# Scan over sequence states: a part of the inflow products on GpSimd, and their decays in PSUM

## The chip, the cores and the metric

The program runs on one core of one Trainium2 chip. The metric is the device time of one execution in microseconds. A core has five engines that run their own instruction streams and wait for one another by semaphores: TensorE (PE, with its weight loads as PEld), VectorE (DVE), ScalarE (ACT), GpSimd (POOL) and SyncE (SP), which issues most transfers. All data are fp32. SBUF holds 128 partitions; PSUM has eight banks of 128x512 fp32, which the kernel calls `dense[:, bank, :]`.

## What is computed

The input is x (4 batches, 1024 positions, 1024 channels) and a context (4, 1024, 512). The output is

```
x = x + ssm(ctx, z = layernorm(x))        # state space block
x = x + ffn(layernorm(x))                 # routed experts (top 2 of 8 per batch), then w3
```

The part that matters here is the recurrence of the first block. For each channel e and each of 16 states n, along the 1024 positions t:

```
dA_t    = exp(delta_t * A[e, n])
h_t     = h_(t-1) * dA_t + (delta_t * u_t) * B_t[n]
y_t     = sum over n of h_t * C_t[n]
```

u is a causal convolution of four taps over an input projection, followed by silu. delta is the softplus of a projection of u; B and C are projections of u as well, one row of 1024 positions per state. Then y + D*u is multiplied by silu(z).

## The kernel before, in words

A batch is cut in 16 steps: two halves in time (`th`, 512 positions each) by eight blocks of 128 channels (`j`). A step `g` handles one tile of 128 channels x 512 positions for all 16 states, in eight slots `q` of one pair of states each (2q and 2q+1). The four batches make 64 steps (`g` from 0 to 63) and a tail. The feed-forward work of batch b-1 and the layer norm of the next batch are put into the slots of batch b by a table written out by hand (`Schedule`, lines 61 to 247): each engine's program walks through all slots in order, so the order of the work on an engine is fixed. The diff leaves the table alone.

For each state n of a step the engines do this:

- ScalarE writes `dA = exp(delta*A)` (line 1189) into one of `RA` = 4 buffers in SBUF. It waits until the scan of four states earlier has read that buffer.
- VectorE multiplies `du = delta*u` (a PSUM bank, DU) by the broadcast row of B (`Bb`) into one of two PSUM banks, M0 for even and M1 for odd states (`times_b`, line 1426). In batch 0, ten of the sixteen products are made by TensorE instead; batches 1 to 3 make all sixteen on VectorE.
- VectorE runs the scan over 512 positions (line 1450), from `dA` and the bank, into `h`. In the second half in time it starts from `state`.
- GpSimd multiplies a pair's `h` by `Cb` in place (line 812, once per slot). In the first half it first copies the last column to `state` (line 806).
- TensorE adds the pair into the accumulator bank YT by transposing matmuls (line 905). `h` has three pairs of buffers (`RH`), so the scan of pair q waits until pair q-3 has been summed.

VectorE makes the products of a pair right after the scans of the pair before it. Around that, a step has further work that couples the engines:

- **Convolution.** In slot 1 (slot 2 in the last channel block) ScalarE makes the first tap of the tile ten steps ahead, after the two `dA` of that slot (`tap_one`, lines 1105 to 1115). In the same slot VectorE makes the three other taps (line 1288), the first of them ahead of the slot's scans; it waits for `first_tap`.
- **Delta of the next step.** TensorE makes `v` (line 864) once the last tap has freed bank S. ScalarE runs Abs, Exp and Ln in slot 4 (lines 1133 to 1139); VectorE ends the softplus after the scans of slot 3 (line 1318). GpSimd makes `du_s` = delta*u in slot 4 (line 785), ScalarE copies it to bank DU in slot 7 (line 1145).
- **Gate.** ScalarE normalizes the z tile in slot 3 (line 1204), and in slot 6 loads another activation table, makes silu of u and of z (lines 1121 and 1221) and loads the first table again (line 1156).
- **Experts.** In batches 1 to 3, sixteen slots a batch hold a Gelu of two tiles with a table load ahead and behind (line 1262): slots 0, 2, 4, 6 of steps 5, 6 and 11, slots 4 and 6 of step 10, slots 0 and 2 of step 12. The expert's output is added by VectorE (line 1404) one slot later. Steps are counted within a batch, from 0.
- **w3 and logits.** TensorE's matmuls of lines 1078 and 1055 lie between its other work, most of them in steps 7 to 9 and 12 to 15.

Of the kernel before, what the change touches and what calls it, by code (L numbers as in the profile page):

```python
# [17 lines left out]
N = 16  # L18
# [19 lines left out]
PE_PAIRS = (1, 2, 4, 5, 6)  # L38
TAIL = 240
# [213 lines left out]
def build(nc, x, ctxT, w_inT, conv_w, conv_b, x_projT, dt_projT, dt_b, A_log, D, sw, sw_b,  # L253
# [4 lines left out]
    with ExitStack() as ctx:  # L258
# [43 lines left out]
        duT = sb("duT", [P, 2, TB, P])  # L302
        h = sb("h", [P, 2 * RH, T])
# [104 lines left out]
        duB_pe_done = sem("duB_pe_done")  # L408
        dA_done = sem("dA_done")
# [65 lines left out]
        def vec_index(g, n):  # L475

            return N * g + n - pe_index(g, n)
# [64 lines left out]
        def _(sync):  # L542
# [77 lines left out]
            def reload_bc(g, c, q):  # L620

                if q == 0:
                    e.wait_ge(bc_stored, 1 + 16 * (c + 1))
                e.wait_ge(duB_done, 1 + vec_index(g, 2 * q + 2))
                e.wait_ge(duB_pe_done, 1 + pe_index(g, 2 * q + 2))
                e.wait_ge(prod_done, 1 + 1 + PAIRS * g + q + 1)
                load_bc(c, q)

            def slot(b, t):
# [31 lines left out]
                for what, *a in PLAN.slots[b][t]:  # L661
# [9 lines left out]
                    elif what == "tail_row":  # L671
                        k = a[0]
                        if k >= 2:
                            e.wait_ge(duB_done, 1 + vec_index(ALL - 1, 2 * (k - 1)))
                        load_x1(tail_rows[k], tail_row_loaded[k], NB - 1, TB + 2 + k if k < 2 else k - 2)
# [6 lines left out]
                    elif what == "sw_load":  # L682
# [60 lines left out]
        def _(pool):  # L743
# [36 lines left out]
            def du_of(g, delta_ready):  # L780
# [11 lines left out]
            def slot(b, t):  # L792
# [7 lines left out]
                if b < NB:  # L800
# [13 lines left out]
                    if q == 4 and g + 1 < ALL:  # L814
                        du_of(g + 1, 1 + count(b, "v", st) + 1)
                    if st == STEPS - 2 and q == 4 and b + 1 < NB:
                        edges(b + 1)
# [266 lines left out]
        def _(act):  # L1084
# [89 lines left out]
            def slot(b, t):  # L1174
# [5 lines left out]
                if b < NB:  # L1180
# [18 lines left out]
                    if q == 3:  # L1199
# [8 lines left out]
                    if q == 4 and g + 1 < ALL:  # L1208
# [60 lines left out]
        def _(dve):  # L1269
# [90 lines left out]
            def slot(b, t):  # L1360
# [77 lines left out]
                for n in (2 * q, 2 * q + 1):  # L1438
                    if on_pe(g, n):
                        e.wait_ge(duB_pe_done, 1 + pe_index(g, n) + 1)  # L1440
                    else:
# [8 lines left out]
                    e.tensor_tensor_scan(h[:, 2 * ((PAIRS * g + q) % RH) + n % 2, :], dA[:, (N * g + n) % RA, :], dense[:, product_bank(g, n), :],  # L1450
# [120 lines left out]
```

## Time and profile before

| | us |
|---|---|
| median of 3 runs | 2517.73 (2517.63 to 2517.95) |
| the profiled execution, its own time | 2518.56 |
| its span in the trace | 2516.8 |
| VectorE busy | 2157.6 (86%) |
| TensorE busy | 2025.6 (80%) |
| ScalarE busy | 1545.5 (61%) |
| GpSimd busy | 1444.6 (57%) |

Batch 1 begins at 562.5 us of the span (first scan of step 16), batch 2 at 1157.5, batch 3 at 1746.5; the last step ends near 2290.3, and the tail takes the rest. Busy times are of instructions from start to end; consecutive instructions of VectorE and ScalarE overlap by about a tenth of a microsecond, so the distance between two starts (the pitch) is what one costs in a full queue.

### The profile page before, as it was taken

The numbers are of one execution on the slowest core, as the hardware profiler recorded it, in microseconds if no ns is written. First come the engines' busy times: TensorE is split into PE (matmuls) and PEld (weight loads), VectorE is DVE, ScalarE is ACT, GpSimd is POOL, SyncE is SP. The second block draws the span as 40 slices with busy tenths as digits, with TensorE's granted clock in tenths as the row PEclk, the third lists the DMA queues.
The fourth block names the chain that finished last, engine by engine and source line by source line (L and its number), as shares of the span: only waits on it lengthen the run. The fifth ranks groups of instructions, "written<-read, shape, count | busy, mean of one in ns | idle before, by whom it ended". The sixth has DMA issues, their size and how long they took to land.

```text
span 2516.8 us, 32784 instructions
## 1 busy us (share of the span) xinstructions
PE 2025.6 (80%) x10840; PEld 1205.0 (48%) x10840; DVE 2157.6 (86%) x2788; ACT 1545.5 (61%) x2237; POOL 1444.6 (57%) x990
## 2 busy tenths in 40 slices
PE   6797889976757897996757897897676897895899
PEld 2676676654433553544433454454443454453244
DVE  5899899979998899989999999998999899994210
ACT  2676566656658569645658658855677768852500
POOL 0687677767755556656756655664675566663000
PEclk9899999997878999997878998998787998997799
DMA  5312425564613744566632554565541264566411
GB/s 172 126 43 84 131 72 167 168 193 158 235 35 109 232 155 144 162 210 205 224 111 84 180 173 134 175 206 181 209 168 63 75 214 152 180 218 242 168 59 67
DMA packets 200186, 382.76 MB, mean 152 GB/s; under 512 B 31537, under 2 KB 97073, under 8 KB 200018
## 3 DMA queue, kind: packets, MB, share of 16 engines
q1 hardware_dynamic: 196848, 380.21, 46.0%
q8 instruction: 87, 1.43, 0.2%
q10 hardware_dynamic: 3170, 0.47, 0.1%
q14 instruction: 81, 0.66, 0.1%
HBM read 346.53 MB, written 34.08 MB: 151 GB/s over the span
## 4 chain that ended last, share of the span: by engine, by line
PE 41%; DVE 21%; issue 18%; ACT 13%; POOL 3%; DMA 2%; DVEq 0%; SPq 0%; ACTq 0%; POOLq 0%
PE dense L1078 13%; DVE h L1450 9%; PE dense L905 8%; PE dense L843 5%; ACT dA L1189 4%; DVE dense L1426 4%; PE dense L891 3%; POOL h L812 3%; DVE u L1288 2%; PE dense L855 2%; ACT L1156 2%; PE dense L1008 2%; PE dense L912 2%; ACT L1262 2%; PE dense L864 2%
## 5 line engine op out<-in xcount | busy, mean ns | idle before, releaser
L812 POOL TENSOR_TENSOR h<-h,Cb 128x1024 f32<-128x1024 f32 x512 | 1208.5, 2361 | 429.8 <-DVE h L1450 405.7
L1189 ACT ACTIVATE dA<-delta,Av 128x512 f32<-128x512 f32 x1024 | 705.4, 717 | 449.3 <-DVE h L1450 446.4
L905 PE MATMUL dense<-ident,h 128*128 128x128 f32 x4096 | 602.8, 298 | 179.0 <-POOL h L812 177.6
L905 PEld LDWEIGHTS dense<-ident,h 128*128 128x128 f32 x4096 | 518.4, 154 | 330.5 <-POOL h L812 240.0
L1450 DVE TENSOR_TENSOR_SCAN h<-dA,state,dense 128x512 f32<-128x512 f32 x512 | 628.4, 1267 | 30.5 <-issue 13.4
L1450 DVE TENSOR_TENSOR_SCAN h<-dA,dense 128x512 f32<-128x512 f32 x512 | 597.3, 1205 | 16.5 <-PE dense L905 8.0
L1426 DVE TENSOR_TENSOR dense<-dense,Bb 128x512 f32<-128x512 f32 x864 | 551.9, 685 | 1.6
L1078 PE MATMUL dense<-w3h,xT 128*128 128x512 f32 x832 | 388.9, 601 | 0.0
L806 POOL COPY state<-h 128x2 f32<-128x2 f32 x256 | 47.6, 186 | 356.1 <-DVE h L1450 354.6
L891 PE MATMUL dense<-Bb,duT 128*128 128x128 f32 x1280 | 181.0, 289 | 48.6 <-DVE h L1450 40.6
L1078 PEld LDWEIGHTS dense<-w3h,xT 128*128 128x128 f32 x832 | 148.6, 194 | 129.0 <-issue 129.0
L843 PE MATMUL dense<-ctxs,win 128*128 128x512 f32 x432 | 209.1, 629 | 1.2 <-ACT dtw L1128 0.7
L891 PEld LDWEIGHTS dense<-Bb,duT 128*128 128x128 f32 x1280 | 160.6, 198 | 80.3 <-issue 74.3
L864 PE MATMUL dense<-dtaug,dtw 33*128 33x512 f32 x128 | 91.3, 800 | 112.3 <-DVE u L1288 110.6
L1288 DVE SCALAR_TENSOR_TENSOR u<-dense,cw,u 128x511 f32<-128x511 f32 (+2 forms) x192 | 140.9, 734 | 41.9 <-ACT u L1106 22.7
L1156 ACT ACT_TABLE_LOAD x113 | 145.0, 1283 | 2.0
L1412 DVE TENSOR_TENSOR res<-dense,res 128x512 f32<-128x512 f32 x64 | 44.0, 687 | 118.1 <-PE dense L1078 117.9
L843 PEld LDWEIGHTS dense<-ctxs,win 128*128 128x128 f32 x432 | 84.2, 204 | 100.8 <-issue 100.8
L1008 PE MATMUL dense<-hs,w2s 128*64 128x512 f32 x224 | 74.7, 740 | 45.0 <-ACT hs L1262 44.2
L1055 PE MATMUL dense<-sww,row 128*32 128x256 f32 x1336 | 109.9, 413 | 1.2 <-ACT row L1230 1.0
L1145 ACT COPY dense<-du_s 128x512 f32<-128x512 f32 x64 | 37.6, 587 | 107.3 <-DVE dense L1426 107.3
L864 PEld LDWEIGHTS dense<-dtaug,dtw 33*128 33x128 f32 x128 | 23.1, 225 | 141.1 <-issue 140.9
(151 smaller groups left out, 2035.6 us busy)
## 6 DMA issues: line engine op xcount, KB each, us to landing
sww<-in_sw SPq DMA_DIRECT2D x170, 512.0 KB, 4.3
Cb<-bc_scratch SPq DMA_DIRECT2D x64, 512.0 KB, 5.7
Bb<-bc_scratch SPq DMA_DIRECT2D x54, 512.0 KB, 4.4
w3h<-in_sw SPq DMA_DIRECT2D x54, 512.0 KB, 8.5
w3h<-in_w3T SPq DMA_DIRECT2D x52, 512.0 KB, 5.1
row<-x_scratch SPq DMA_DIRECT2D x42, 512.0 KB, 4.9
xz<-in_x SPq DMA_DIRECT2D x64, 256.0 KB, 5.0
xt<-in_x SPq DMA_DIRECT2D x64, 256.0 KB, 4.1
```

Source lines behind the costliest of these rows:

```text
L812: e.tensor_tensor(h[:, s:s + 2, :], h[:, s:s + 2, :], Cb[:, 2 * q:2 * q + 2, :], ALU.mult).then_inc(prod_done, 1)
L843: mm = e.matmul(dense[:, bank, :], win[:, par, k, :], ctxs[:, k, :], start=(k == 0), stop=(k == DK - 1))
L864: e.matmul(dense[:, S, :], dtw[0:DR + 1, j * P:(j + 1) * P], dtaug[:], start=True, stop=True) \
L891: mm = e.matmul(dense[:, product_bank(g, n), k * P:(k + 1) * P], duT[:, g % 2, k, :], Bb[:, n, k * P:(k + 1) * P], start=True, stop=True)
L905: mm = e.matmul(yT[:, k, :], h[:, 2 * ((PAIRS * g + q) % RH) + i, k * P:(k + 1) * P], ident[:], is_transpose=True, start=False, stop=(q == ...
L1008: mm = e.matmul(dense[HD * i:HD * i + HD, bank, :], w2s[:], hs_of(b, hp)[:, i, :], start=True, stop=True)
L1078: mm = e.matmul(dense[:, bank, :], xT_of(b, uu)[:, d, k * P:(k + 1) * P], w3[:, d, :], start=False, stop=(d == J - 1), skip_group_check=True)
L1156: e.preload_act_table_set("natural_log_exp_and_others")
L1189: e.activation(dA[:, i % RA, :], delta[:, st % 2, :], ACT.Exp, scale=Av[:, j * N + n:j * N + n + 1]).then_inc(dA_done, 1)
L1288: i = e.scalar_tensor_tensor(out=u[:, G % UR, s:T], in0=dense[:, bank, 0:T - s], scalar=cw[:, j, k:k + 1], in1=u[:, G % UR, s:T], op0=ALU. ...
L1426: e.tensor_tensor(dense[:, product_bank(g, n), :], du[:], Bb[:, n, :], ALU.mult).then_inc(duB_done, 1)
L1450: e.tensor_tensor_scan(h[:, 2 * ((PAIRS * g + q) % RH) + n % 2, :], dA[:, (N * g + n) % RA, :], dense[:, product_bank(g, n), :], state[:, ...
```

## The change

It touches batches 1 to 3 (`g >= STEPS`). For the odd state of pairs 0, 1, 2, 4 and 7 (states 1, 3, 5, 9 and 15) of each step:

- the product du*B is made by GpSimd from `du_s` (SBUF) into `duB_s`, two SBUF tiles that batch 0 uses as `duT`. It is issued some slots ahead: after the C product of slots 0, 2, 4, 6, 7 for pairs 2, 4, 7 and the next step's 0 and 1;
- ScalarE writes `dA` of this state into PSUM bank M1 instead of an SBUF buffer, and waits for the scan two states earlier to be done, the last reader of that bank;
- the scan reads its decay from the bank and its inflow from `duB_s`;
- the ring of four `dA` buffers is used by the eleven other states alone.

In batches 1 to 3 GpSimd makes `du_s` in slot 5 instead of 4, ScalarE normalizes z in slot 2 instead of 3, and runs Abs, Exp, Ln in slot 3 instead of 4.

```diff
+POOLED = (0, 1, 2, 4, 7)
+AHEAD_POOLED = {0: 2, 2: 4, 4: 7, 6: 8, 7: 9}
...
+def pooled(g, n):
+    return g >= STEPS and n % 2 == 1 and n // 2 in POOLED
...
+        duB_s = duT[:].rearrange("p i k e -> p i (k e)")
...
 @block.gpsimd
+            def times_b(g, q):
+                n, i = 2 * q + 1, pool_index(g, 2 * q + 1)
+                if g % J == 0:
+                    e.wait_ge(bc_loaded[q], bc_value(g // J, q))
+                if i < 2:
+                    e.wait_ge(duB_pe_done, 1 + pe_index(STEPS - 1 + i, 0))
+                else:
+                    k, m = divmod(i - 2, len(POOLED))
+                    e.wait_ge(h_done, 1 + N * (STEPS + k) + 2 * POOLED[m] + 2)
+                e.tensor_tensor(duB_s[:, i % 2, :], du_s[:], Bb[:, n, :], ALU.mult).then_inc(duB_s_done, 1)
...
-                    if q == 4 and g + 1 < ALL:
+                    if q == (5 if b else 4) and g + 1 < ALL:
                         du_of(g + 1, 1 + count(b, "v", st) + 1)
+                    ahead = divmod(PAIRS * g + AHEAD_POOLED[q], PAIRS) if q in AHEAD_POOLED else (ALL, 0)
+                    if STEPS <= ahead[0] < ALL:
+                        times_b(*ahead)
...
 @block.scalar
                     for n in (2 * q, 2 * q + 1):
-                        i = N * g + n
-                        if i >= RA:
-                            e.wait_ge(h_done, 1 + i - RA + 1)
-                        e.activation(dA[:, i % RA, :], delta[:, st % 2, :], ACT.Exp,
+                        if pooled(g, n):
+                            e.wait_ge(h_done, 1 + N * g + n - 1)
+                            dst = dense[:, M1, :]
+                        else:
+                            i = ring_index[g, n]
+                            if i >= RA:
+                                before = in_ring[i - RA]
+                                e.wait_ge(h_done, 1 + N * before[0] + before[1] + 1)
+                            dst = dA[:, i % RA, :]
+                        e.activation(dst, delta[:, st % 2, :], ACT.Exp,
                                      scale=Av[:, j * N + n:j * N + n + 1]).then_inc(dA_done, 1)
...
-                    if q == 3:
+                    if q == (2 if b else 3):
...
-                    if q == 4 and g + 1 < ALL:
+                    if q == (3 if b else 4) and g + 1 < ALL:
...
 @block.vector
+                    elif pooled(g, n):
+                        i = pool_index(g, n)
+                        e.wait_ge(duB_s_done, 1 + i + 1)
+                        decay, inflow = dense[:, M1, :], duB_s[:, i % 2, :]
...
-                        if not on_pe(g, n):
+                        if not on_pe(g, n) and not pooled(g, n):
                             times_b(g, n)
```

SyncE's reloads of `Bb` also wait for `duB_s_done`, and `du_of` waits until the products of its step have been read out of `du_s`.

ScalarE's order at the start of the second step of batch 1, from the `dA` of slot 0 to the normalized z tile. Before:

```order
L1189 ACTIVATE dA<-delta,Av 128x512 [waits h_done,evac0]
L1189 ACTIVATE dA<-delta,Av 128x512 [waits h_done]
L1195 ACTIVATE uD<-u,Dv 128x512 [waits prod_summed]
L1189 ACTIVATE dA<-delta,Av 128x512 [waits h_done] x2
L1112 ACTIVATE u<-dense,edge,cw 128x1 [waits u_done,xin_done,du_s_done]
L1112 ACTIVATE u<-dense,edge,cw 128x1 x2
L1115 ACTIVATE u<-dense,cb,cw 128x509
L1189 ACTIVATE dA<-delta,Av 128x512 [waits h_done] x4
L1204 ACTIVATE xz<-xz,nm,r 128x512 [waits xz_loaded]
```

And now, the same place (`dense<-delta,Av` is the decay that goes to bank M1):

```order
L1230 ACTIVATE dA<-delta,Av 128x512 [waits h_done,evac0]
L1230 ACTIVATE dense<-delta,Av 128x512 [waits h_done]
L1236 ACTIVATE uD<-u,Dv 128x512 [waits prod_summed]
L1230 ACTIVATE dA<-delta,Av 128x512 [waits h_done]
L1230 ACTIVATE dense<-delta,Av 128x512 [waits h_done]
L1147 ACTIVATE u<-dense,edge,cw 128x1 [waits u_done,xin_done,du_s_done]
L1147 ACTIVATE u<-dense,edge,cw 128x1 x2
L1150 ACTIVATE u<-dense,cb,cw 128x509
L1230 ACTIVATE dA<-delta,Av 128x512 [waits h_done]
L1230 ACTIVATE dense<-delta,Av 128x512 [waits h_done]
L1245 ACTIVATE xz<-xz,nm,r 128x512 [waits xz_loaded]
```

The first tap still stands behind the slot's second decay. That decay now goes to the bank, and the z tile has moved ahead of the decays of slot 3.

VectorE at the same place, from the scans of slot 0 to the gate product of slot 2 (a scan is printed as SCALAR_TENSOR_TENSOR with `h` as its output). Before:

```order
L1450 SCALAR_TENSOR_TENSOR h<-dA,dense 128x512 [waits prod_summed,dA_done,duB_done]
L1450 SCALAR_TENSOR_TENSOR h<-dA,dense 128x512 [waits dA_done,duB_done]
L1426 TENSOR_TENSOR dense<-dense,Bb 128x512 [waits h_done,du_done] x2
L1288 SCALAR_TENSOR_TENSOR u<-dense,cw,u 128x511 [waits conv_step,first_tap]
L1450 SCALAR_TENSOR_TENSOR h<-dA,dense 128x512 [waits prod_summed,dA_done,duB_done]
L1288 SCALAR_TENSOR_TENSOR u<-dense,cw,u 128x510 [waits conv_step]
L1450 SCALAR_TENSOR_TENSOR h<-dA,dense 128x512 [waits dA_done,duB_done]
L1288 SCALAR_TENSOR_TENSOR u<-dense,cw,u 128x509 [waits conv_step]
L1426 TENSOR_TENSOR dense<-dense,Bb 128x512 [waits h_done,du_done] x2
L1370 TENSOR_TENSOR szT<-dense,szT 128x512 [waits prod_summed,evac0]
```

And now (`h<-dense,duT` is a scan that reads its decay from M1 and its inflow from GpSimd's tile):

```order
L1496 SCALAR_TENSOR_TENSOR h<-dA,dense 128x512 [waits prod_summed,dA_done,duB_done]
L1496 SCALAR_TENSOR_TENSOR h<-dense,duT 128x512 [waits dA_done,duB_s_done]
L1467 TENSOR_TENSOR dense<-dense,Bb 128x512 [waits h_done,du_done]
L1329 SCALAR_TENSOR_TENSOR u<-dense,cw,u 128x511 [waits conv_step,first_tap]
L1496 SCALAR_TENSOR_TENSOR h<-dA,dense 128x512 [waits prod_summed,dA_done,duB_done]
L1329 SCALAR_TENSOR_TENSOR u<-dense,cw,u 128x510 [waits conv_step]
L1496 SCALAR_TENSOR_TENSOR h<-dense,duT 128x512 [waits dA_done,duB_s_done]
L1329 SCALAR_TENSOR_TENSOR u<-dense,cw,u 128x509 [waits conv_step]
L1467 TENSOR_TENSOR dense<-dense,Bb 128x512 [waits h_done,du_done]
L1411 TENSOR_TENSOR szT<-dense,szT 128x512 [waits prod_summed,evac0]
```

One product of each pair is gone here, and one product alone stands between the second scan and the first of VectorE's taps.

GpSimd in slots 3 to 5 of that step. Before:

```order
L799 TENSOR_TENSOR xt<-szT,xt 128x512 [waits yg_done,xt_loaded]
L806 COPY state<-h 128x2 [waits h_done]
L812 TENSOR_TENSOR h<-h,Cb 128x1024 [waits saved]
L806 COPY state<-h 128x2 [waits h_done]
L812 TENSOR_TENSOR h<-h,Cb 128x1024 [waits saved]
L785 TENSOR_TENSOR du_s<-delta,u 128x512 [waits du_turned,du_done,evac0]
L806 COPY state<-h 128x2 [waits h_done,du_s_done]
L812 TENSOR_TENSOR h<-h,Cb 128x1024 [waits saved]
```

And now (`duT<-du_s,Bb` is a product for a scan some slots later):

```order
L831 TENSOR_TENSOR xt<-szT,xt 128x512 [waits yg_done,xt_loaded]
L838 COPY state<-h 128x2 [waits h_done]
L844 TENSOR_TENSOR h<-h,Cb 128x1024 [waits saved]
L838 COPY state<-h 128x2 [waits h_done]
L844 TENSOR_TENSOR h<-h,Cb 128x1024 [waits saved]
L818 TENSOR_TENSOR duT<-du_s,Bb 128x512 [waits h_done]
L838 COPY state<-h 128x2 [waits h_done]
L844 TENSOR_TENSOR h<-h,Cb 128x1024 [waits saved]
L805 TENSOR_TENSOR du_s<-delta,u 128x512 [waits du_turned,duB_s_done,du_done,evac0]
```

The product stands where `du_s` stood, and `du_s` has moved one slot back. Four more such products stand in the other slots.

## Rows read from the trace of the kernel before

**Rows 1.** The page: busy per engine, then the costliest groups, times and means

```profile
PE 2025.6 (80%) x10840; PEld 1205.0 (48%) x10840; DVE 2157.6 (86%) x2788; ACT 1545.5 (61%) x2237; POOL 1444.6 (57%) x990
L812 POOL TENSOR_TENSOR h<-h,Cb 128x1024 f32<-128x1024 f32 x512 | 1208.5, 2361 | 429.8 <-DVE h L1450 405.7
L1450 DVE TENSOR_TENSOR_SCAN h<-dA,state,dense 128x512 f32<-128x512 f32 x512 | 628.4, 1267 | 30.5 <-issue 13.4
L1450 DVE TENSOR_TENSOR_SCAN h<-dA,dense 128x512 f32<-128x512 f32 x512 | 597.3, 1205 | 16.5 <-PE dense L905 8.0
L1426 DVE TENSOR_TENSOR dense<-dense,Bb 128x512 f32<-128x512 f32 x864 | 551.9, 685 | 1.6
```

**Rows 2.** Windows, batches 1 to 3: length; busy PE, PEld, DVE, ACT, POOL; clock; DMA

```profile
562.50:1157.50 595.00, 471.87 (x2372) 265.66 (x2372) 558.08 (x729) 392.45 (x563) 361.06 (x246) 0.87 0.50 164
1157.50:1746.50 589.00, 469.63 (x2372) 264.73 (x2372) 558.05 (x729) 392.30 (x563) 361.11 (x246) 0.88 0.50 166
1746.50:2290.30 543.80, 423.08 (x2274) 243.44 (x2274) 524.14 (x666) 372.68 (x521) 357.03 (x240) 0.88 0.47 154
```

**Rows 3.** Windows of single steps: batch 2 steps 1, 5, 11, 13, 14; batch 3 step 13

```profile
1189.80:1222.10 32.30, 22.36 (x154) 14.67 (x154) 32.20 (x44) 19.12 (x28) 22.49 (x23) 0.79 0.31 105
1331.60:1370.20 38.60, 24.66 (x114) 12.49 (x114) 36.72 (x50) 35.58 (x48) 22.80 (x18) 0.91 0.35 125
1554.60:1593.40 38.80, 30.15 (x178) 14.80 (x178) 36.16 (x48) 34.91 (x46) 22.04 (x13) 0.91 0.49 150
1629.70:1664.20 34.50, 34.50 (x191) 17.81 (x191) 34.40 (x45) 18.57 (x26) 22.05 (x13) 1.00 0.57 172
1664.20:1702.60 38.40, 38.40 (x186) 19.26 (x185) 32.95 (x40) 19.19 (x30) 23.73 (x15) 1.00 0.60 202
2194.40:2226.90 32.50, 30.36 (x174) 16.00 (x174) 32.40 (x42) 17.59 (x24) 21.95 (x13) 1.00 0.56 181
```

**Rows 4.** Timeline, VectorE, batch 2 step 1: start, length, line, idle before

```profile
1189.84 2.32 DVE L1450 TENSOR_TENSOR_SCAN h<-dA,dense 128x512 f32<-128x512 f32 x2
1192.07 1.27 DVE L1426 TENSOR_TENSOR dense<-dense,Bb 128x512 f32<-128x512 f32 x2
1193.25 0.74 DVE L1288 SCALAR_TENSOR_TENSOR u<-dense,cw,u 128x511 f32<-128x511 f32 x1
...
1204.89 0.67 DVE L1318 SCALAR_TENSOR_TENSOR delta<-dense,delta 128x512 f32<-128x512 f32 x1
1205.60 1.30 DVE L1426 TENSOR_TENSOR dense<-dense,Bb 128x512 f32<-128x512 f32 x2
```

**Rows 5.** Timeline, ScalarE, same step: taps, then a decay

```profile
1188.52 0.81 ACT L1112 ACTIVATE u<-dense,edge,cw 128x1 f32<-128x1 f32 x3
1189.23 0.76 ACT L1115 ACTIVATE u<-dense,cb,cw 128x509 f32<-128x509 f32 x1
1191.08 0.72 ACT L1189 ACTIVATE dA<-delta,Av 128x512 f32<-128x512 f32 x1 [1.09 <-DVE h L1450]
```

**Rows 6.** Timeline, ScalarE, batch 2 step 11: first Gelu's table load, next decays

```profile
1553.91 1.28 ACT L1262 ACT_TABLE_LOAD   x1
...
1557.78 1.34 ACT L1189 ACTIVATE dA<-delta,Av 128x512 f32<-128x512 f32 x2
```

**Rows 7.** Timeline, VectorE, same step: its first tap

```profile
1559.88 0.75 DVE L1288 SCALAR_TENSOR_TENSOR u<-dense,cw,u 128x511 f32<-128x511 f32 x1 [1.04 <-ACT u L1106]
```

**Rows 8.** Waits of VectorE, batches 1 to 3: total us, times, longest

```profile
DVE delta L1318 <- ACT delta L1139: 17.3, 5, 3.8
```

**Rows 9.** Timeline, GpSimd, batch 2 step 1: an SBUF product of 512

```profile
1204.21 1.29 POOL L799 TENSOR_TENSOR xt<-szT,xt 128x512 f32<-128x512 f32 x1
1205.43 0.19 POOL L806 COPY state<-h 128x2 f32<-128x2 f32 x1
```

**Rows 10.** Timeline around 1145 us, end of batch 1

```profile
1145.04 2.35 POOL L812 TENSOR_TENSOR h<-h,Cb 128x1024 f32<-128x1024 f32 x1
1145.10 2.31 DVE L1311 SCALAR_TENSOR_TENSOR nm<-mv,r 128x8 f32<-128x8 f32 x1 [0.70 <-POOL r L755]
```

More of the change, by code:

```diff
@@ L408, in build @@
         duB_pe_done = sem("duB_pe_done")
+        duB_s_done = sem("duB_s_done")
         dA_done = sem("dA_done")
@@ L475, in vec_index, with pool_index @@
         def vec_index(g, n):
-            return N * g + n - pe_index(g, n)
+            return N * g + n - pe_index(g, n) - pool_index(g, n)
+        def pool_index(g, n):
+            return len(POOLED) * max(g - STEPS, 0) + sum(pooled(g, m) for m in range(n))
+        in_ring = [(g, n) for g in range(ALL) for n in range(N) if not pooled(g, n)]
+        ring_index = {gn: i for i, gn in enumerate(in_ring)}
         def bank_free(g, n):
@@ L625, in reload_bc @@
                 e.wait_ge(duB_pe_done, 1 + pe_index(g, 2 * q + 2))
+                e.wait_ge(duB_s_done, 1 + pool_index(g, 2 * q + 2))
                 e.wait_ge(prod_done, 1 + 1 + PAIRS * g + q + 1)
@@ L674, in slot @@
                             e.wait_ge(duB_done, 1 + vec_index(ALL - 1, 2 * (k - 1)))
+                            e.wait_ge(duB_s_done, 1 + pool_index(ALL - 1, 2 * (k - 1)))
                         load_x1(tail_rows[k], tail_row_loaded[k], NB - 1, TB + 2 + k if k < 2 else k - 2)
@@ L703, in slot @@
                             e.wait_ge(duB_done, 1 + vec_index(ALL - 1, n))
+                            e.wait_ge(duB_s_done, 1 + pool_index(ALL - 1, n))
                         dst, done, _ = sw_tile(b, k, i)
@@ L1438, in slot @@
                 for n in (2 * q, 2 * q + 1):
+                    decay, inflow = dA[:, ring_index.get((g, n), 0) % RA, :], dense[:, product_bank(g, n), :]
                     if on_pe(g, n):
                         e.wait_ge(duB_pe_done, 1 + pe_index(g, n) + 1)
+                    elif pooled(g, n):
+                        i = pool_index(g, n)
+                        e.wait_ge(duB_s_done, 1 + i + 1)
+                        decay, inflow = dense[:, M1, :], duB_s[:, i % 2, :]
                     else:
@@ L1449, in slot @@
                         e.wait_ge(saved, 1 + PAIRS * (J * (b + 1)))
-                    e.tensor_tensor_scan(h[:, 2 * ((PAIRS * g + q) % RH) + n % 2, :], dA[:, (N * g + n) % RA, :], dense[:, product_bank(g, n), :],
+                    e.tensor_tensor_scan(h[:, 2 * ((PAIRS * g + q) % RH) + n % 2, :], decay, inflow,
                                          state[:, j * N + n:j * N + n + 1] if th else 0.0, ALU.mult, ALU.add) \
@@ L1466, in slot @@
                     for n in (0, 1):
-                        times_b(g + 1, n)
+                        if not pooled(g + 1, n):
+                            times_b(g + 1, n)
                 if j == J - 1 and g + 1 < STEPS and q and on_pe(g + 1, 2 * (q - 1)):
```

1 line of the change is left out of this document (added).

## The prediction

> **What bounds the kernel now.** I read the page first, then the windows of the batches, then single steps, then the timelines of VectorE and ScalarE inside one step. The page makes VectorE the busiest engine, but over a span with a tail in which it does little [rows 1]. In the windows of batches 1 to 3 it is busy for 558.1 of 595.0, 558.1 of 589.0 and 524.1 of 543.8 us, 94 to 96%; ScalarE has 66 to 69% and GpSimd 61 to 66% [rows 2]. The reader should not stop at that mean, because the steps differ [rows 3]. In a plain step (batch 2, step 1) VectorE is busy for 32.2 of 32.3 us and ScalarE for 19.1. In an expert step ScalarE nearly ties: 35.6 of 38.6 and 34.9 of 38.8. In steps 13 and 14 TensorE is busy for all of 34.5 and 38.4 us. So an edit that relieves VectorE pays in plain steps, and elsewhere runs into the next engine soon.
>
> **What goes.** Two products begin at 1192.07 and the next instruction at 1193.25, so one costs 0.59 us in the queue, though its own length is 0.69 [rows 1, 4]. Five a step over 48 steps are 240 products, 141.6 us. Part comes back. A pair's two products used to separate each product from its scan. With one left in pairs 0, 4 and 7 the scan waits for the instruction just ahead (pairs 1 and 2 have a tap or the gate product between). What that costs is seen where a product waits for the delta just written: 0.67 long, next start after 0.71 instead of about 0.59 [rows 4]. I take 0.11 for each, 0.33 a step. VectorE alone would save 2.6 us a step, 126 us in 48 steps.
>
> **The scan's new operands.** No row shows a scan with its decay in PSUM and its inflow in SBUF; it has one operand of each kind as before. Bounds: nothing, or the 0.06 that the form with a state operand costs over the plain one (1267 against 1205 ns) [rows 1], on 240 scans 14 us either way. I take nothing.
>
> **The new wait, and what is queued behind it.** The decay of an odd pooled state may begin when the scan two states back is done; before, it could run four states ahead. Taken alone that is harmless: VectorE then makes a product (0.59, and 0.11) and a scan (1.12, from 1189.84 to 1192.07 for two) before it wants the decay, 1.8 us, and the decay takes 0.72 and some 0.04 to start [rows 4, 5]. About 1.0 us of slack is left. But ScalarE is a queue, and two things go wrong.
>
> First, the tap. ScalarE's first tap stands behind the decay of state 3, which now waits for scan 1. VectorE wants this tap one product later, after 0.59. ScalarE needs 0.62 for the decay (two take 1.34, one 0.72), 0.71 for the three column pieces, 0.76 for the rest and some 0.06 to start and hand over, 2.15 in all [rows 4 to 6]. VectorE stands for 1.6 us. Where the tile ten steps ahead belongs to the first half in time there are no column pieces, and it stands for 0.9. Before, the same tap was ready more than 2 us early in a plain step (1189.23 + 0.76, wanted at 1193.25, is 3.3) [rows 4, 5]. Convolution ends at step 6 of batch 3, so 39 of the 48 steps have it. In steps 0 to 6 and 15 it is the 1.6.
>
> A plain step (0 to 4) thus gains 2.6 - 1.6 = 1.0; 15 such steps give 15 us.
>
> Second, the experts' Gelu. From its first table load to the next decay it takes 1557.78 - 1553.91 = 3.87 us [rows 6], far over the slack of 1.0. In step 11 I lay out ScalarE's queue from scan 0 at time 0. Decay 1 ends by -0.05, `uD` by 0.6, the Gelu by 4.5, decays 2 and 3 by 5.7, the tap by 6.5; VectorE took that tap at 1559.88 - 1554.56 = 5.3 before [rows 7], so it is 1.2 late. Decay 5 then waits for scan 3 (10.1), z 11.4, Gelu 15.3, decays 6 and 7 16.5, the softplus 18.4. Decay 9 waits for scan 7 (20.5), Gelu 25.0, decays 10 to 13 27.4, silu and both table loads 31.2, a norm 32.4, Gelu 36.3, decays 14 and 15 37.5. VectorE adds the expert's output near 36.5 to 37.1, runs two scans and a product, and starts the next step at about 40.2, against 38.8 now. ScalarE has 34.9 of work, and its two waits for scans put 4.5 us of idle into the queue. So this step loses 1.5 us. Steps 5 and 6 of batches 1 and 2 have statistics on VectorE (1.8 us) in slots 0 and 4, which give ScalarE room; the same walk gives 38.0 against 38.6. I take 0.25 gained there and 0.5 lost in batch 3. Step 10 comes out even; step 12, with two Gelus, gains 0.7, and 1.5 in batch 3. Gelu steps together: -2.2 us, with 5 lost in step 11.
>
> **TensorE.** Steps 8, 9, 13 and 14 of batches 1 and 2 are full on TensorE as the two shown are [rows 3], so VectorE's saving turns into waiting for sums or tiles: 1 us in all eight. In batch 3 there is less projection work and step 13 leaves 2.1 us free; with steps 8, 9 and 14 I count 5. Steps 7 and 15 have a wait of VectorE for delta, up to 3.8 us [rows 8], whose chain starts at TensorE; what VectorE saves ahead of it is lost there, what comes behind is kept: 6 us in the six.
>
> **GpSimd.** A product of this form costs it 1.22 from start to start [rows 9], so 6.1 a step. On 22.5 busy, with some 1.3 of gaps between its copies and products, that is 29.9 of the 31.3 that a plain step then takes [rows 3]. It fits, but it runs late in slots 4 to 0: 3.9 us a pair against 3.2 of VectorE. The product for the next step's state 1 is ready 4.8 us after scan 13, wanted at 4.8. The C products come up to 3 us late, and a scan wants their sum two pairs on, so this is covered, and slot 1 with its taps lets GpSimd catch up. I take 0; if the cover is gone it is up to 1 us in each of the 24 first-half steps.
>
> **Sum.** 15 + 1 + 5 + 6 - 2.2 = 24.8 us, of the 126 that VectorE alone would give. The tail follows the last scan unchanged. The profiled execution took 2518.56 us (span 2516.8), 0.8 over the median of 2517.73. 2518.6 - 24.8 = 2493.8, and at the median 2493.
>
> **A lock that would speak against it.** At 1145.10 VectorE's product of 128x8 elements takes 2.31 us; it ends at 1147.41, as GpSimd's product of 1145.04 + 2.35 = 1147.39 does [rows 10]. Both its inputs, `mv1` and `r1`, lie in SBUF. The scans, with one of them in PSUM, keep to 1.2 us beside the same product. The Trainium skill ("SBUF — State Buffer", Who interferes with whom) says that a VectorE instruction with two SBUF inputs contends with a GpSimd instruction that reads SBUF, as a lock for a whole instruction. The row agrees, and by this rule the pooled scans are free, because their decay lies in PSUM.
>
> **Rivals.**
>
> *A. The waits mostly hide.* If the tap is not late, or its stall only uses up idle time that other steps have anyway, plain steps gain 2.6 (15 x 1.6 = 24 us more) and the expert steps lose nothing (9 steps, some 14 us): 2493 - 38 = 2455. For it: VectorE is the bound in most steps. Against: the order leaves the tap behind the waiting decay. 0.17.
>
> *B. ScalarE becomes the bound, slower.* Place: the fifteen expert steps. Each of the two or three decays that wait for a scan puts 1.5 to 3 us of idle into a queue that is 92% busy. If VectorE's additions of the expert output come late as well, as the Gelu now starts later, all Gelu slots pay: 42 of them at 0.8 us, 35 us more than I count, and nothing hides it: 2493 + 35 = 2528. It decides from the point where ScalarE's work ahead of a waiting decay exceeds 1.0 us. For it: 3.87 against 1.0. Against: some Gelus already start late now, for TensorE's reasons. 0.20.
>
> *C. GpSimd late.* The 24 first-half steps lose the 1.0 they gain and as much in the loaded ones: 2493 + 15 = 2508. For it: 29.9 of 31.3. Against: the slack of two pairs. 0.10.
>
> *D. The scans contend after all.* A pooled scan that waited half a GpSimd product (1.2 us), 240 times, would add 280: 2773. Rows 10 and the scans beside it speak against. 0.02.
>
> **How the numbers follow.** Forecast 0.51. A measurement of this kernel tells 0.2%, 5 us, from no change. Faster by more: most of the forecast, A, half of C: 0.70. Within: a little of the forecast, of B and C: 0.10. Slower: most of B, D: 0.20. The range goes from A's 2455 to B's 2528.
>
> **What would show it.** Right: VectorE waits before its first tap (line 1288, now 1329) for ScalarE's first tap 0.9 to 1.6 us in nearly every step with a convolution; plain steps of 31.3; step 11 near 40; steps 9, 13 and 14 of batches 1 and 2 unchanged; scans unchanged in length; GpSimd busy for 290 us more. Wrong: plain steps near 29.7 (A), or expert steps of 41 and more (B), or VectorE waiting for GpSimd's products (C).

## The result, and the profile after

The changed kernel takes 2531.72 us (median of 4 runs, 2526.52 to 2532.72) against 2517.68 us for the kernel before on the same chips: a ratio of 1.0053, 95% interval 1.0036 to 1.0070. It is slower by 0.5%. The forecast was 2493 us, with 0.20 given to slower and 2528 as the upper end of the range.

The page of the changed kernel, engine totals and the groups that answer to [rows 1]:

```profile
PE 2034.4 (81%) x10840; PEld 1212.7 (48%) x10840; DVE 2032.7 (81%) x2548; ACT 1535.7 (61%) x2237; POOL 1732.5 (69%) x1230
L844 POOL TENSOR_TENSOR h<-h,Cb 128x1024 f32<-128x1024 f32 x512 | 1207.5, 2359 | 287.6 <-DVE h L1496 262.4
L818 POOL TENSOR_TENSOR duT<-du_s,Bb 128x512 f32<-128x512 f32 x240 | 305.4, 1273 | 0.0
L1230 ACT ACTIVATE dense<-delta,Av 128x512 f32<-128x512 f32 x240 | 165.4, 689 | 408.2 <-DVE h L1496 407.8
L1496 DVE TENSOR_TENSOR_SCAN h<-dense,state,duT 128x512 f32<-128x512 f32 x120 | 151.2, 1260 | 0.0
L1496 DVE TENSOR_TENSOR_SCAN h<-dense,duT 128x512 f32<-128x512 f32 x120 | 144.1, 1201 | 1.3 <-POOL duT L818 1.3
```

The work moved as the change says. VectorE is busy for 125 us less, GpSimd for 288 us more, and the scans have kept their length with the new operands (1201 and 1260 ns). The row to stop at is that of line 1230: ScalarE stands idle for 408 us ahead of its 240 decays for bank M1, waiting for scans. Before, all 1024 decays together had 449 us of such idle time.

The windows of the three batches, as in [rows 2]:

```profile
560.00:1154.40 594.40, 472.55 (x2372) 267.10 (x2372) 516.11 (x648) 389.03 (x563) 457.12 (x326) 0.88 0.49 164
1154.40:1751.70 597.30, 474.00 (x2372) 267.99 (x2372) 516.03 (x648) 389.13 (x563) 457.13 (x326) 0.87 0.49 163
1751.70:2298.20 546.50, 430.53 (x2274) 249.20 (x2274) 483.58 (x587) 372.11 (x526) 451.17 (x318) 0.87 0.46 153
```

The batches take 594, 597 and 547 us (595, 589, 544 before) with 42 us less VectorE work in each of the first two. The third window ends 0.5 us ahead of the end of the last scan, where that of [rows 2] ends 1.0 us behind it, so like for like batch 3 is at 548. Steps 1, 5, 11, 13 and 14 of batch 2, as in [rows 3]:

```profile
1186.30:1218.30 32.00, 21.28 (x146) 14.06 (x146) 29.75 (x40) 20.13 (x31) 28.40 (x26) 0.79 0.35 130
1326.70:1367.80 41.10, 27.06 (x114) 13.96 (x114) 34.04 (x44) 34.44 (x47) 30.50 (x24) 0.83 0.34 118
1555.40:1596.70 41.30, 30.03 (x178) 14.30 (x178) 33.59 (x42) 34.98 (x46) 28.11 (x18) 0.92 0.46 141
1635.50:1670.50 35.00, 35.00 (x194) 17.97 (x193) 31.96 (x39) 18.70 (x28) 27.12 (x18) 1.00 0.56 183
1670.50:1710.10 39.60, 39.60 (x189) 19.79 (x188) 30.32 (x35) 19.41 (x30) 30.87 (x21) 1.00 0.59 200
```

The plain step gains 0.3 us, the two expert steps (5 and 11) lose 2.5 each, and steps 13 and 14, full on TensorE, lose 0.5 and 1.2. Step lengths, from the first scan of a step to the first scan of the next (for the last step to the end of its last scan), give the account for the two traces (us against before, batches 1 to 3 together, a minus is a gain):

| steps | forecast | the change |
|---|---|---|
| 0 to 4 | -15 | -4.0 |
| 5, 6, 10, 11, 12 (expert) | +2.2 | +27.9 |
| 8, 9, 13, 14 | -6 | -2.9 |
| 7, 15 | -6 | -9.3 |
| sum | -25 | +11.8 |

In the profiled execution batch 1 also begins 2.5 us earlier and the tail is 1.4 shorter, so its span is 7.9 us longer; its own time, 2526.52, is the lowest of the four, 5 us below the median, so the table holds 8 of the 14 us that the medians are apart.

What VectorE waited for in batches 1 to 3, as in [rows 8]:

```profile
DVE xT L1445 <- PE dense L1043: 51.4, 38, 2.9
DVE h L1496 <- PE dense L940: 44.5, 39, 2.6
DVE u L1329 <- ACT u L1150: 34.6, 23, 2.1
DVE h L1496 <- ACT dA L1230: 25.8, 17, 7.4
...
DVE u L1329 <- ACT u L1141: 12.8, 14, 1.4
...
DVE h L1496 <- POOL duT L818: 1.3, 3, 0.4
```

Before, these rows had 7.6 (expert output), 7.5 (sums), 7.6, 4.2 (decays) and 3.9 us. The row of decays is not like for like: it holds two waits of 7.4 us ahead of step 15, which before stood at the same places under "issue" with 5.9 and 5.4 us. The first tap costs 47 us in 37 waits; the forecast's 1.6 and 0.9 us in 39 steps come to 51. Twice that lies in two rows that the forecast had priced at little: the expert's output (line 1043) and the sums of pairs (line 940), both from TensorE. The first lies in the expert steps. Of the second 14.2 us do; the other 30 are in other steps. GpSimd's products are waited for 3 times.

How a plain step loses its gain, in batch 2, step 1, VectorE from scan 0 to the scans of states 6 and 7 (starts and lengths as in [rows 4]):

```profile
1186.30 1.21 DVE L1496 TENSOR_TENSOR_SCAN h<-dA,dense 128x512 f32<-128x512 f32 x1
1187.42 1.20 DVE L1496 TENSOR_TENSOR_SCAN h<-dense,duT 128x512 f32<-128x512 f32 x1
1188.54 0.68 DVE L1467 TENSOR_TENSOR dense<-dense,Bb 128x512 f32<-128x512 f32 x1
1190.80 0.75 DVE L1329 SCALAR_TENSOR_TENSOR u<-dense,cw,u 128x511 f32<-128x511 f32 x1 [1.59 <-ACT u L1150]
...
1200.16 2.33 DVE L1496 TENSOR_TENSOR_SCAN h<-dA,dense 128x512 f32<-128x512 f32 x2 [0.45 <-PE dense L940]
```

TensorE in the same stretch:

```profile
1195.23 2.04 PE L899 MATMUL dense<-dtaug,dtw 33*128 33x512 f32 x2 [4.40 <-DVE u L1329]
1197.21 1.11 PE L985 MATMUL dense<-ident,uD 128*128 128x128 f32 x4
1198.12 3.19 PE L940 MATMUL dense<-ident,h 128*128 128x128 f32 x14
```

The tap wait is the 1.6 of the forecast. The 0.45 is new: the last tap releases `v` (two passes, 2.04 us after an idle stretch of TensorE, with a granted clock of 0.50 there, the lower level of 1.2 GHz), then `uD` and the sum of pair 0 follow, and scan 6 needs that sum. Before, `v` took the same 2.04 us and nobody waited. The product of state 5, now gone from VectorE, used to cover this.

### The profile page after: what moved, and what is told of

It is laid out like the page before. It is cut to its first block, busy times and chain, and to the rows that moved or that the text cites. A ratio compares the mean times of both kernels' runs of the same rounds, so it can differ in the third digit from the quotient of the medians.

```text
span 2524.7 us, 32693 instructions
## 1 busy us (share of the span) xinstructions
PE 2034.4 (81%) x10840; PEld 1212.7 (48%) x10840; DVE 2032.7 (81%) x2548; ACT 1535.7 (61%) x2237; POOL 1732.5 (69%) x1230
## 4 chain that ended last, share of the span: by engine, by line
PE 43%; DVE 17%; issue 17%; ACT 14%; POOL 6%; DMA 2%; SPq 0%; DVEq 0%; ACTq 0%; POOLq 0%
PE dense L1113 14%; PE dense L940 9%; DVE h L1496 8%; PE dense L878 4%; POOL h L844 4%; PE dense L926 3%; ACT dA L1230 2%; ACT L1303 2%; PE dense L890 2%; DVE dense L1467 2%; DVE u L1329 2%; PE dense L1090 2%; ACT L1191 2%; PE dense L1043 2%; ACT hs L1303 2%
## 5 line engine op out<-in xcount | busy, mean ns | idle before, releaser
L940 PE MATMUL dense<-ident,h 128*128 128x128 f32 x4096 | 613.8, 302 | 158.2 <-POOL h L844 158.1
L940 PEld LDWEIGHTS dense<-ident,h 128*128 128x128 f32 x4096 | 529.3, 157 | 312.1 <-POOL h L844 207.6
L1230 ACT ACTIVATE dA<-delta,Av 128x512 f32<-128x512 f32 x784 | 538.4, 715 | 142.9 <-DVE h L1496 140.9
L1496 DVE TENSOR_TENSOR_SCAN h<-dA,state,dense 128x512 f32<-128x512 f32 x392 | 486.0, 1268 | 57.6 <-ACT dA L1230 26.8
L1496 DVE TENSOR_TENSOR_SCAN h<-dA,dense 128x512 f32<-128x512 f32 x392 | 461.7, 1206 | 37.3 <-PE dense L940 23.8
L1230 ACT ACTIVATE dense<-delta,Av 128x512 f32<-128x512 f32 x240 | 165.4, 689 | 408.2 <-DVE h L1496 407.8
L1467 DVE TENSOR_TENSOR dense<-dense,Bb 128x512 f32<-128x512 f32 x624 | 407.4, 681 | 1.6
L818 POOL TENSOR_TENSOR duT<-du_s,Bb 128x512 f32<-128x512 f32 x240 | 305.4, 1273 | 0.0
L926 PE MATMUL dense<-Bb,duT 128*128 128x128 f32 x1280 | 180.5, 289 | 48.3 <-DVE h L1496 40.2
L1496 DVE TENSOR_TENSOR_SCAN h<-dense,state,duT 128x512 f32<-128x512 f32 x120 | 151.2, 1260 | 0.0
L1496 DVE TENSOR_TENSOR_SCAN h<-dense,duT 128x512 f32<-128x512 f32 x120 | 144.1, 1201 | 1.3 <-POOL duT L818 1.3
```

Of the source, the lines that this page charges most:

```text
L818: e.tensor_tensor(duB_s[:, i % 2, :], du_s[:], Bb[:, n, :], ALU.mult).then_inc(duB_s_done, 1)
L926: mm = e.matmul(dense[:, product_bank(g, n), k * P:(k + 1) * P], duT[:, g % 2, k, :], Bb[:, n, k * P:(k + 1) * P], start=True, stop=True)
L940: mm = e.matmul(yT[:, k, :], h[:, 2 * ((PAIRS * g + q) % RH) + i, k * P:(k + 1) * P], ident[:], is_transpose=True, start=False, stop=(q == ...
L1230: e.activation(dst, delta[:, st % 2, :], ACT.Exp, scale=Av[:, j * N + n:j * N + n + 1]).then_inc(dA_done, 1)
L1467: e.tensor_tensor(dense[:, product_bank(g, n), :], du[:], Bb[:, n, :], ALU.mult).then_inc(duB_done, 1)
```

## The experiments

Each kernel was timed against the kernel before on the same chip. Twelve were run.

**e1, the tap between the two decays.**

```diff
 for n in (2 * q, 2 * q + 1):
     ... decay of state n
+    if n == 2 * q and b and late(b, t, conv_slot(st)) and G < ALL:
+        tap_one(G, S, *chunk_block(G))        # was behind both decays
```

> The changed kernel (2531.7 us), but in the slot of the convolution ScalarE makes its first tap between the two decays instead of behind both, in batches 1 to 3. Theory S (what ScalarE's queue holds behind a waiting decay is late, place by place): VectorE's wait before its first tap (47 us in 37 waits, 1.6 in a plain step) goes; a plain step falls from 32.0 to about 30.4, and the steps full on TensorE give nothing; with the fifteen plain steps at 1.6 and about 1 us in each of the other steps that have it, 2531.7 - 35 = 2497. Rival Q (ScalarE's queue as a whole is the bound, so an earlier tap only makes decay 3 late): within 4 us of 2531.7. Rival G (GpSimd's later products are the hidden bound of plain steps): VectorE waits for GpSimd's products or for the sums behind them instead, 2520 or more.

2501.51 us, ratio 0.9940 (0.9927 to 0.9954). The same place as above, batch 2 step 1:

```profile
1176.90 0.67 DVE L1471 TENSOR_TENSOR dense<-dense,Bb 128x512 f32<-128x512 f32 x1
1177.48 0.74 DVE L1333 SCALAR_TENSOR_TENSOR u<-dense,cw,u 128x511 f32<-128x511 f32 x1
```

The tap follows without a gap. The step takes 30.3 us, and decay 3 is in time. VectorE's waits ahead of its first tap fall from 47 to 9 us. One moved call turns the change from slower into faster than before. Steps 0 to 4 stand at -28.0 us, the expert steps still at +22.5.

**e2, no pooling in the expert steps.** `pooled` is false for steps 5, 6, 10, 11, 12; waits and indices follow.

> The changed kernel, but no state is pooled in steps 5, 6, 10, 11 and 12 of batches 1 to 3, where ScalarE has the Gelus; there all decays stay in the ring of four and VectorE makes all products. Theory S: these fifteen steps cost 28 us more than before the change in the profile, from Gelus behind waiting decays, and now return to their old times (38.6, 38.2, 35.5, 38.8, 36.4 in batch 2): 2531.7 - 28 = 2504. Rival G (GpSimd late everywhere): it is less loaded in five of sixteen steps, the others keep the loss: about 2525. If the loss of these steps comes from the slots that were moved (z, softplus, du) and not from the decays, they stay near 41 us: 2530.

2493.12 us, ratio 0.9902 (0.9887 to 0.9918), 39 us below the changed kernel, 11 more than expected. The expert steps go from +27.9 to -2.7, and the steps full on TensorE (8, 9, 13, 14) from -2.9 to -6.9; most of the rest is that the 28 was read from a profiled execution 5 us below its median.

**e3, both.**

> Both edits together: first tap between the decays, and no pooling in steps 5, 6, 10, 11 and 12. Theory S: the two losses are at different places and add: 2504 less 1.6 in fifteen plain steps and about 0.9 in the ten others with a convolution that are not full on TensorE, 2504 - 30 = 2474, below the kernel before (2517.7). Rival Q: no more than the second edit alone, 2504. Rival G: 2515.

2470.87 us, ratio 0.9816 (0.9802 to 0.9829). The two losses are at different places and nearly add (30 and 39 us alone, 61 together). Step 5 of batch 2 is back at 38.0, step 11 at 37.6.

**e4, GpSimd's products one column wide**, the inflow of the pooled states left out.

> The changed kernel, but GpSimd's 240 products are one column wide instead of 512, so the inflow of the pooled states is left out; all waits, decays and scans are as in the change. It prices GpSimd's added work alone. Theory S: GpSimd is covered except for small waits at the ends of steps 2 and 3: 2531.7 less 5 or fewer. Rival G: its C products come 1 to 2.4 us later than before in the changed kernel, and the scans that wait for their sums lose that: 20 to 30 us come back, 2505.

2519.87 us, ratio 1.0011 (1.0002 to 1.0021). GpSimd's work costs 12 us, not 5. In the profile 6.6 of it lie in steps 0 to 4, most in step 2 (33.0 against 34.7): in the changed kernel a scan near its start waits 0.42 us for GpSimd's product, and the first scan of step 3 waits 1.19 us for a sum. The cost is real, but a fifth of the 61 us that the change loses against e3.

**e5, the decays of the pooled states in the SBUF ring.**

```diff
-    if pooled(g, n):
-        e.wait_ge(h_done, 1 + N * g + n - 1)
-        dst = dense[:, M1, :]
+    # all sixteen states in the ring of four, as before
...
-    decay, inflow = dense[:, M1, :], duB_s[:, i % 2, :]
+    decay, inflow = dA[:, ring_index[g, n] % RA, :], duB_s[:, i % 2, :]
```

> The changed kernel (2531.7), but ScalarE writes all sixteen decays into the SBUF ring of four, as before the change; GpSimd still makes the five products a step. So ScalarE's lead of four states is back and the waiting decay is gone, while the pooled scan has both inputs in SBUF. Without a contention for ports the waits that theory S names vanish: expert steps back to 38 us, plain steps 30.3: about 2531.7 - 35 - 30 = 2467 or less. With a lock of a whole instruction (a VectorE instruction with two SBUF inputs against a GpSimd product), GpSimd is busy some 80% of the step, and a pooled scan waits on average 1 us for the product under way, or makes it wait: 240 scans, up to 240 us on top, 2467 + 100 to 240 = 2570 to 2710, and the pooled scans show lengths over 1.27 us.

2554.41 us, ratio 1.0146 (1.0129 to 1.0163). Direction right, size below the range. With the waiting decay gone and GpSimd's products kept, the expert steps stand at -6.9 us against the kernel before, so they do not lose by the products. But the pooled scans and GpSimd's products are longer:

```profile
L818 POOL TENSOR_TENSOR duT<-du_s,Bb 128x512 f32<-128x512 f32 x240 | 398.1, 1659 | 0.0
L1493 DVE TENSOR_TENSOR_SCAN h<-dA,duT 128x512 f32<-128x512 f32 x120 | 228.3, 1902 | 3.2 <-POOL duT L818 3.2
L1493 DVE TENSOR_TENSOR_SCAN h<-dA,state,duT 128x512 f32<-128x512 f32 x120 | 199.8, 1665 | 0.0
```

Against the other scans of the same kernel (1205 and 1266) this is 0.70 and 0.40 us each, 132 us of VectorE, and 0.39 for each GpSimd product, 93 us. The timeline shows one turn of it:

```profile
1190.74 2.34 POOL L844 TENSOR_TENSOR h<-h,Cb 128x1024 f32<-128x1024 f32 x1
1192.71 1.45 DVE L1493 TENSOR_TENSOR_SCAN h<-dA,duT 128x512 f32<-128x512 f32 x1
1193.04 2.20 POOL L818 TENSOR_TENSOR duT<-du_s,Bb 128x512 f32<-128x512 f32 x1
```

GpSimd's product ends at 1193.08 and the scan 1.08 us later, at 1194.16, which fits a scan that is held until the product ends; the next GpSimd product, started at 1193.04, takes 2.20 instead of 1.27. The Trainium skill ("SBUF — State Buffer", Who interferes with whom) says that a VectorE instruction with two SBUF inputs contends with a GpSimd instruction that reads SBUF, and one with at most one SBUF input does not. [rows 10] showed it for one small product; here the trace agrees for the scan, 1902 and 1665 ns with two SBUF inputs against 1201 and 1260 ns with one of them in PSUM in the changed kernel. The wait for the bank is the price of keeping clear of this.

**e6, the moved slots alone**, on the kernel before.

> The kernel before (2517.6) with nothing of the change but the moved slots: in batches 1 to 3 z is normalized in slot 2, softplus runs in slot 3, du_s is made in slot 5. Theory S puts the loss into the waiting decays, so this is within 5 us of 2517.6. If the moved slots carried part of the loss of the expert steps (28 us), it is 2525 to 2545.

2516.12 us, ratio 0.9995 (0.9985 to 1.0004). No difference.

**e7, v behind the first sums**, on e3.

```diff
 # slot 2, batches 1 to 3
-before_softplus(...)          # v
 first_sum(g)                  # uD, sum of pair 0
+before_softplus(...)
 sum_pair(g, 1)
```

> As e3 (2470.9: tap between the decays, expert steps unpooled), and in slot 2 TensorE makes v (the next step's delta projection) behind the first sums of the step instead of ahead of them. Theory V: the 0.45 us wait of the scan of state 6 in plain steps is the end of a chain, last tap, v (two passes of 1.02 us at the lower clock), uD, sum of pair 0, which one product fewer on VectorE no longer covers; with v behind, the wait goes in the plain steps and shrinks in the others (33.6 us of waits of scans for line 940's sums in all, of which a third): 2471 - 10 = 2461. Rival W: the softplus, which waits for v, comes late by as much, and VectorE waits at delta instead: 2471 or more.

2494.51 us, 24 above e3. Rival W held. Batch 2 step 1, where the scans of states 6 and 7 no longer wait:

```profile
1188.37 2.32 DVE L1504 TENSOR_TENSOR_SCAN h<-dA,dense 128x512 f32<-128x512 f32 x2
1191.96 0.69 DVE L1367 SCALAR_TENSOR_TENSOR delta<-dense,delta 128x512 f32<-128x512 f32 x1 [1.27 <-ACT delta L1178]
```

The 0.45 is gone, so its chain was read rightly, and 1.27 stands before delta instead. `v` has two followers, the sums behind it and the softplus, and neither has room. Of the 24 us, 13.6 lie in the expert steps and 6.7 in steps 0 to 4.

**e8 and e10, which decays cost in the expert steps**, on e3: pairs 0, 1, 7 pooled there, then pairs 2 and 4.

> As e3, but in the expert steps pairs 0, 1 and 7 are pooled as well, pairs 2 and 4 not. In the changed kernel ScalarE stood idle 3.1 us ahead of decay 5 and 2.1 us ahead of decay 9 in these steps, then had a Gelu behind them. If these two waits carry the loss, the expert steps stay near e3's (38 us) or gain the 1.8 us of three products where ScalarE allows it: 2471 - 5 to + 8. If any waiting decay in an expert step costs (the queue as a whole has no room), three of five carry three fifths of the 28 us: 2488.

> The complement of e8: as e3, but in steps 5, 6, 10, 11 and 12 pairs 2 and 4 alone are pooled. In the profiles these steps sum to -6.0 us against the kernel before with no pair pooled, +4.1 with pairs 0, 1, 7, +22.5 with all five (e1). If the losses are those of single waiting decays and add, pairs 2 and 4 carry 18 us: 2471 + 18 = 2489. If they carry little by themselves and it takes all five to fill the queue: below 2480.

e8 takes 2480.06, ratio 0.9851 (0.9835 to 0.9868); e10 2496.54, ratio 0.9914 (0.9898 to 0.9929): 9 and 26 us over e3, where all five together (e1) cost 31. The expert steps stand at -6.0 with none, +4.1 with 0, 1, 7, +17.6 with 2 and 4, +22.5 with all. So the waits of decays 5 and 9 carry most, and the three others are cheap but not free; e8 ends 1 us above the range expected if only the waits of decays 5 and 9 cost, e10 8 us above the 2489 expected if single losses add. In the changed kernel's fifteen expert steps ScalarE stands 41 us ahead of decay 5 and 35 ahead of decay 9, mostly with a Gelu right behind. Decay 1 often has a Gelu behind it too, but only 11 us of standing ahead of it. Step 10, whose Gelus come late in the step, gains from pairs 0, 1, 7: 34.4 against 36.0.

**e11, the wait alone.** The kernel before, with

```diff
-    e.wait_ge(h_done, 1 + i - RA + 1)
+    e.wait_ge(h_done, 1 + i - (2 if g >= STEPS and n in (1, 3, 5, 9, 15) else RA) + 1)
```

> The kernel before (2517.6) with one thing added: in batches 1 to 3 the decays of states 1, 3, 5, 9 and 15 wait for the scan two states back instead of four. No work moves, nothing goes to PSUM or GpSimd. Theory S: the wait by itself makes the loss. VectorE still makes two products ahead of its tap, 1.18 us, against 2.15 for decay and taps: it stands 1.0 us in each of 15 plain steps; the expert steps lose about as much as in the change plus what its shorter VectorE work gave back there (30 to 40 us); some more in the other steps: 2517.6 + 15 + 35 + 5 = 2572. If instead the loss comes from GpSimd or from the new operands, this stays within 10 us of 2517.6.

2658.04 us, ratio 1.0559 (1.0543 to 1.0575), 86 above what was expected. The tap wait of a plain step is 0.99 us, as worked out (0.33 where there are no column pieces). What was missed stands in slot 4, where decay 9 and the softplus follow each other. ScalarE and then VectorE, batch 2 step 1:

```profile
1253.01 0.72 ACT L1189 ACTIVATE dA<-delta,Av 128x512 f32<-128x512 f32 x1 [3.69 <-DVE h L1450]
1253.64 0.58 ACT L1133 ACTIVATE delta<-dense 128x512 f32<-128x512 f32 x1
```

```profile
1255.57 0.69 DVE L1318 SCALAR_TENSOR_TENSOR delta<-dense,delta 128x512 f32<-128x512 f32 x1 [2.60 <-ACT delta L1139]
```

Decay 9 waits for scan 7, the softplus waits behind it, and VectorE, having ended scan 7, waits for the softplus: 2.60 us here, 125 us in 47 of the 48 steps. This is what the moved slots are for.

**e12, the wait and the moved slots.** e11 on e6.

> The kernel before (2517.6) with the waits of e11 (decays of states 1, 3, 5, 9, 15 wait for the scan two states back) and the moved slots of e6 (softplus, z and du), so everything that the change does to the order and the waits, and nothing of the work it moves. e11 came out at 2658, far above its 2572, and its profile has VectorE standing 2.6 us for delta in nearly every step: the softplus of slot 4 was queued behind decay 9, which waits for scan 7. With softplus in slot 3 that wait goes. Theory S: VectorE's tap waits of 1.0 and 0.3 us stay, plain steps are 33.3, expert steps 40: 2517.6 + 15 + 24 + 5, about 2560. If the slots do not cure it, 2620 or more; if the waits cost nothing once the slots are moved, 2520.

2561.23 us, ratio 1.0173 (1.0156 to 1.0190), as expected in sum. This splits the change in two: its order and waits cost 43.5 us over the kernel before, and the work that it takes off VectorE gives back 29.5. The expert steps stand at +32.4 (24 was expected) with no work moved at all.

**e9, pooled pairs chosen by step**, on e3: all five in steps 0 to 4, 7, 8, 13, 15; pairs 0, 1, 2, 7 in step 10; 4 and 7 in step 12; 7 in steps 5, 6, 11; none in 9 and 14.

> As e3 (2470.9: tap between the decays), with the pooled pairs chosen step by step in batches 1 to 3: all five in steps 0 to 4, 7, 8, 13 and 15; pairs 0, 1, 2, 7 in step 10; 4 and 7 in step 12; 7 alone in steps 5, 6 and 11 (its decay stands behind the last Gelu, where scan 13 is done anyway); none in steps 9 and 14. Theory S, place by place: step 10 falls from 36.0 to 34.4 as in e8, steps 9 and 14 of batch 2 from 36.9 and 39.6 to 34.8 and 38.3 as before the change, step 12 gives up to 1: 2471 - 5 to 12, so 2462. If TensorE's queue takes these up again (its work is the same), 2469 to 2473.

2464.14 us, ratio 0.9786 (0.9773 to 0.9800). The fastest of all, 2.1% below the kernel before and 2.7% below the change. Steps 10 and 12 of batch 2 are at 34.7 and 34.3. Steps 9 and 14 did not return to their old times (36.4 and 39.6 in batch 2, 34.8 and 38.3 before) though nothing is pooled there. TensorE is full in that stretch; that it arrives with more of its queue undone is a guess that was not tried.

## Why the prediction was wrong

**Bound and saving.** The bound was read rightly, and so was the saving: 0.59 us for each of 240 products, less 0.11 for some of them, 126 us on VectorE's queue (its busy time fell by 125).

**The tap.** Right in place and size: 1.59 forecast as 1.6 in steps 0 to 3, 0.93 as 0.9 in steps 9, 10, 13 and 14 (steps 4, 6 and 15 had 1.1 to 1.2, step 5 had 2.1). e1 took most of it away and gave 30 us.

**The plain step** was forecast to gain 1.0 and gained 0.3, steps 0 to 4 together 4 instead of 15. A part is the 0.45 of the chain over `v`. The prediction did not walk this chain: VectorE had never waited there, and that slack was partly the product that went. Another part is GpSimd, which was priced at nothing: it comes late at step 2, and e4 measures 12 us in all.

**The step that failed is the experts' Gelu**: "Gelu steps together: -2.2 us", where the minus is a loss. The loss measured is 27.9 us (the +27.9 of the table above). That is 25.7 of the 37 us between the forecast's sum and the profile's; the plain steps are 11. The mechanism was named (a Gelu of 3.87 us queued ahead of or behind a waiting decay), and the walk through step 11 came to 40.2, measured 41.3. The size of the term failed, and most in the steps that were not walked:

| steps | forecast | the change |
|---|---|---|
| 5, 6 | 0 | +13.9 |
| 10 | 0 | +3.2 |
| 11 | +5 | +7.4 |
| 12 | -2.9 | +3.5 |

"The same walk gives 38.0" for steps 5 and 6; they took 41.2 and 41.9 in batch 2. Batch 2 step 5 of the changed kernel, ScalarE from the waiting decay to the Gelu, then TensorE, then VectorE:

```profile
1336.06 0.69 ACT L1230 ACTIVATE dense<-delta,Av 128x512 f32<-128x512 f32 x1 [3.11 <-DVE h L1496]
...
1338.80 1.26 ACT L1303 ACTIVATE hs<-dense,b1s 128x512 f32<-128x512 f32 x2
```

```profile
1336.81 2.04 PE L899 MATMUL dense<-dtaug,dtw 33*128 33x512 f32 x2 [5.24 <-DVE u L1329]
1340.16 1.98 PE L1043 MATMUL dense<-hs,w2s 128*64 128x512 f32 x4 [1.31 <-ACT hs L1303]
1342.07 1.12 PE L985 MATMUL dense<-ident,uD 128*128 128x128 f32 x4
1342.98 2.67 PE L940 MATMUL dense<-ident,h 128*128 128x128 f32 x16
```

```profile
1342.17 0.75 DVE L1445 SCALAR_TENSOR_TENSOR xT<-dense,b2s,xT 128x512 f32<-128x512 f32 x1 [0.89 <-PE dense L1043]
1344.91 2.33 DVE L1496 TENSOR_TENSOR_SCAN h<-dA,dense 128x512 f32<-128x512 f32 x2 [1.99 <-PE dense L940]
```

The Gelu is late because decay 5 waited 3.1 us for scan 3. From there the delay reaches VectorE in two ways. The direct one: the expert's output (line 1043) waits for the Gelu, and VectorE, which adds it, waits for that. The other goes through TensorE's queue, which the walk took as free: the sum of pair 0 stands behind the expert's output, so scan 6 waits 2 us, and the next waiting decay is later still. VectorE waits 5.2 us more in this step than before: 1.1 for the tap, 2.1 for outputs and 2.0 for this sum. Step 11 has no wait for sums; there it is the outputs (1.7, 0.8 and 2.6 us). Over all fifteen steps the waits for outputs are 51.4 us against 7.6 before, and those for sums 14.2 against 4.1; with nothing pooled there (e2) they are 12.5 and 5.2.

It was rival B, "ScalarE becomes the bound", that described it, with 0.20 and 2528 us: Gelus that start late, and VectorE's additions late with them. It priced this at 35 us more than was counted (42 slots at 0.8, which is 34); 25.7 was measured, and the plain steps make up most of the rest of the way to 2531.72. Its condition, more than 1.0 us of ScalarE's work ahead of a waiting decay, was met in all fifteen steps. What was held against it was that some Gelus start late anyway. They came later still: in batch 2 step 5 the second one started 7.6 us after scan 0 before, and 12.1 now.

The steps full on TensorE together gained 2.9 us of the 6 forecast, but not step by step: step 8 gained 6.5, step 9 lost 2.7 and step 14 lost 1.7, where about nothing was forecast for steps 9 and 14 in batches 1 and 2. Why step 9 loses is open. Steps 7 and 15, forecast at 6 us, gained 9.3.

Rival A fell with the tap. Rival C has its 12 us. Rival D is excluded by the scans' lengths, and e5 shows the contention with both inputs in SBUF.

## What to carry to other kernels

When an instruction in an engine's queue gets a later condition, price everything that stands behind it in that queue, and then walk every queue that waits for those instructions, TensorE's too, until the delay comes back to where it began; e12 shows that the wait alone can cost more than the moved work returns. Put work that others wait for ahead of the waiting instruction (one moved call gave 30 us here), and apply such a change only in the stretches where the engine that takes the wait has room (another 31 to 39 us). A slack read from the old trace is partly made of the work one is about to remove.

## What the runs showed of the hardware

- A scan with its decay in PSUM and its inflow in SBUF takes 1201 ns, as with the operands the other way round (1206). With both in SBUF beside a busy GpSimd it takes 1902 on average, up to 3377, and GpSimd's product of 128x512 takes 1659 instead of 1273 (e5).
- An exponential of 128x512 takes ScalarE 689 ns to PSUM and 715 ns to SBUF, in the same kernel.
- A VectorE scan directly behind the product that it reads starts 0.70 to 0.74 us after that product starts. An instruction that does not read it starts 0.58 to 0.60 us after.
